# First-layer attention on one Trainium2 core: the four high and low products as 64-row pairs of heads, the folded causal mask, value products in twos

## The reference

```python
latent_kv = x @ w_kv_down                    # (4, 1024, 128)
kv = latent_kv @ w_kv_up                     # k and v, 16 heads of 64
q = (x @ w_q).reshape(Bx, Tx, 16, 64)
att = jnp.einsum('bqhd,bkhd->bhqk', q, k) * 64 ** -0.5
att = jnp.where(causal, att, -jnp.inf)
att = jax.nn.softmax(att, axis=-1)
y = jnp.einsum('bhqk,bkhd->bqhd', att, v)
return y.reshape(Bx, Tx, 1024) @ w_out
```

## Time and profile before

| | |
|---|---|
| median of 3 runs | 2570.04 us (2569.2 to 2572.35) |
| the profiled execution | 2569.28 us, its span 2567.5 us |
| PE busy in the span | 2312.1 us, 90% |
| DVE busy | 1850.8 us, 72% |
| ACT busy | 1497.5 us, 58% |
| granted TensorE clock, mean | 0.961 |

### The profile page before, as it was taken

The page is one execution under the profiler, slowest core; times in us unless marked ns, Lnnn a source line. Parts: engine busy times, 40 slices in busy tenths (PEclk is TensorE's granted clock), DMA queues, the critical chain, the costliest instruction groups (busy, mean ns, idle before and its releaser), DMA issues. The chain is left out here.

```text
span 2567.5 us, 46435 instructions
## 1 busy us (share of the span) xinstructions
PE 2312.1 (90%) x17339; PEld 1338.3 (52%) x17339; DVE 1850.8 (72%) x2346; ACT 1497.5 (58%) x2293; POOL 125.4 (5%) x256
## 2 busy tenths in 40 slices
PE   3799999999999999999999955859999999999998
PEld 2466666666565666666566632624444444444444
DVE  8677777777777777777777775067777777777781
ACT  3465666657575656666575731306666566566666
POOL 0100000000000000000000021000000000000000
PEclk8899999999999999999999977959999999999999
DMA  2000000000000000000000008033111110112000
GB/s 75 1 0 0 0 0 0 0 0 0 0 0 0 0 0 0 0 0 0 0 0 0 0 17 194 11 45 63 18 18 20 34 26 18 27 19 32 12 2 10
DMA packets 41099, 41.16 MB, mean 16 GB/s; under 512 B 21392, under 2 KB 33632, under 8 KB 40864
## 3 DMA queue, kind: packets, MB, share of 16 engines
q1 hardware_dynamic: 38904, 36.87, 7.2%
q10 hardware_dynamic: 1448, 1.61, 0.4%
q0 software_dynamic: 640, 1.15, 0.4%
HBM read 26.60 MB, written 11.63 MB: 15 GB/s over the span
## 5 line engine op out<-in xcount | busy, mean ns | idle before, releaser
L1462 DVE TENSOR_REDUCE nm_half<-slot 128x2 f32<-128x1024 f32 x512 | 605.2, 1223 | 188.4 <-PE slot L1311 146.2
L1444 ACT ACTIVATE pT<-slot 128x1024 f32<-128x1024 f32 x512 | 506.2, 1027 | 332.0 <-PE slot L1394 278.7
L573 ACT ACTIVATE probT<-slot 128x1024 f32<-128x1024 f32 x192 | 171.0, 890 | 326.9 <-PE slot L474 326.9
L474 PEld LDWEIGHTS slot<-ident,prob 128*128 128x128 f32 x2304 | 245.7, 141 | 198.6 <-issue 166.8
L610 DVE TENSOR_REDUCE negmax<-slot 128x1 f32<-128x896 f32 (+7 forms) x416 | 282.5, 708 | 76.4 <-PE slot L464 76.4
L474 PE MATMUL slot<-ident,prob 128*128 128x128 f32 x2304 | 328.0, 281 | 2.1
L486 PE MATMUL yspace<-probT,v_sb 128*64 128x512 f32 (+3 forms) x1536 | 318.3, 507 | 0.0
L1306 PE MATMUL slot<-ks,qs 48*128 48x512 f32 x1024 | 254.3, 495 | 53.6 <-DMA ks<-rows 29.1
L565 ACT ACTIVATE prob<-slot,negmax 128x896 f32<-128x896 f32 (+7 forms) x416 | 292.6, 720 | 9.6 <-DVE negmax L610 9.6
L1360 PE MATMUL yspace<-pT,v 128*32 128x512 f32 x2048 | 267.7, 604 | 1.7 <-ACT y_raw L1431 0.8
L459 PE MATMUL slot<-k_hi,q_st 128*128 128x512 f32 (+3 forms) x608 | 240.8, 396 | 26.4 <-ACT prob L565 11.4
(11 more groups left out here) (240 smaller groups left out, 3007.8 us busy)
## 6 DMA issues: line engine op xcount, KB each, us to landing
qs<-q_hi SPq DMA_DIRECT2D x64, 64.0 KB
qs<-q_lo SPq DMA_DIRECT2D x64, 64.0 KB
ks<-k_hi SPq DMA_DIRECT2D x60, 64.0 KB
ks<-k_lo SPq DMA_DIRECT2D x60, 64.0 KB
x_tok<-in_L_attn_x_dram SPq DMA_DIRECT2D x4, 512.0 KB, 7.4
q_hi<-qk_out SPq DMA_DIRECT2D x4, 512.0 KB, 3.2
q_lo<-qk_out SPq DMA_DIRECT2D x4, 512.0 KB, 4.1
k_hi<-qk_out SPq DMA_DIRECT2D x4, 512.0 KB, 4.2
```

The lines of the kernel that those rows point to most:

```text
L474: last = nc.tensor.transpose(ps[:, a * BANK + j * P:a * BANK + (j + 1) * P], prob[a][:, p_at(4 * c + j, kt)], ident[:, :])
L1444: nc.scalar.activation(pT[hp][m % PT_DEEP][:, :, :], slot[at["x", n] % RING][:, :].rearrange("p (j t) -> p j t", t=BANK), ACT.Exp)\
L1462: nc.vector.tensor_reduce(nm_half[:, h, :, p * TPB + i], slot[pos % RING][:, :].rearrange("p (a t) -> p a t", t=BANK), AX.X, ALU.max, nega ...
```

## The change

The high parts of both heads now stand side by side in one tensor, `q_hl[0]` (rows 0 to 63 head 0, rows 64 to 127 head 1), the low parts in `q_hl[1]`, and `k_hl` in the same way; nothing is doubled. A product of one head is over its own 64 rows, and the matmuls of the two heads are issued one after the other, on the two halves of the array's rows. Four passes (high and low of q with high and low of k) replace two of 128 rows. The mask is folded to 64 rows: `fold` picks and `causal` holds keys in two halves, so a tile's mask is two matmuls of 128 and 64 columns.

The tiles of i = 7 to 4 keep a space each but are computed in twos (both heads together, both spaces claimed first); for i = 3 to 0 both heads share one slot, head a in bank a, with one maximum (L615 of the new kernel) and two exponentials. `s_list` has 12 entries instead of 16; entries 3 and 7 are in `yspace`. LAG is 3, four buffers of `probT`, and products are issued in twos after items 3, 5, 7, 9 and 11 (`GROUP`); S_LEAD and S_PER are 2.

```diff
-                q_st = [sB(f"q_st{a}", [P, T], F32R) for a in range(2)]
-                k_hi2 = [sB(f"k_hi2{a}", [P, T], F32R) for a in range(2)]
-                k_lo2 = [sB(f"k_lo2{a}", [P, T], F32R) for a in range(2)]
+                q_hl = [sB(f"q_hl{r}", [P, T], F32R) for r in range(2)]
+                k_hl = [sB(f"k_hl{r}", [P, T], F32R) for r in range(2)]
...
-                NS = 2 * TPB
-                NS1 = NS // 2
+                s_list = [(i, a) for i in (7, 6, 5, 4) for a in range(2)] + [(i, None) for i in (3, 2, 1, 0)]
+                NS = len(s_list)
+                NS1 = TPB
...
-                LAG = 2
+                LAG = 3
+                GROUP = 2
...
-                S_LEAD, S_PER = 3, 5
+                S_LEAD, S_PER = 2, 2
...
-                Y_TILES = [0, 4, 8]
+                Y_TILES = [3, 7]
...
+                        def scores(n):
+
+                            i, a0 = s_list[n]
                             w = (i + 1) * P
+                            if n == 0:
+
+                                pe.wait_ge(hi_done, 2 * it + 2)
+                                freed(pe, it, TQ)
+                            if a0 is None:
+                                ps = score_claim(n)
+                                own_ps = [ps[:, a * BANK:a * BANK + w] for a in range(2)]
+                            else:
+                                own_ps = [score_claim(n + a)[:, 0:w] for a in range(2)]
+                            for k, (hq, hk) in enumerate(((0, 0), (1, 0), (0, 1), (1, 1))):
+                                if n == 0 and k == 2:
+
+                                    freed(pe, it, TK)
+                                for o in range(0, w, BANK):
+                                    m = min(BANK, w - o)
+                                    for a in range(2):
+                                        own = slice(a * HS, (a + 1) * HS)
+                                        last = nc.tensor.matmul(own_ps[a][:, o:o + m], q_hl[hq][own, i * P:(i + 1) * P], k_hl[hk][own, o:o + m],
+                                                                start=(k == 0), stop=(k == 3 and o + m < w))
+                                        if n == 0 and k == 0 and o == 0 and a == 0:
+
+                                            last.then_inc(proj_done, 1)
+                            for f in range(2):
+                                for a in range(2):
+                                    own = slice(a * HS, (a + 1) * HS)
+                                    last = nc.tensor.matmul(own_ps[a][:, i * P + f * HS:w], fold[own, f, :], causal[own, f, f * HS:P], start=False, stop=(f == 1))
+                                    if f == 1 and (a0 is not None or a == 1):
+                                        last.then_inc(score_space(n + a if a0 is not None else n)[1], 1)
+
+                        for n in range(0, NS1, 2):
                             scores(n)
...
-                            if m >= LAG:
-                                product(m - LAG)
-                        for m in range(NT - LAG, NT):
+                            if m >= LAG and m % GROUP == GROUP - 1:
+                                for k in range(GROUP):
+                                    product(m - LAG + k)
+                        for m in range(NT - LAG + GROUP - 1, NT):
                             product(m)
...
+                        for n, dst in ((TQ, q_hl), (TK, k_hl)):
+                            filled(act, it, n)
+                            nc.scalar.activation(dst[0][:, :], slot[n % RING][:, :], ACT.Copy).then_inc(hi_done, 1)
...
+                            for a, o in ([(a0, 0)] if a0 is not None else [(0, 0), (1, BANK)]):
+                                last = nc.scalar.activation(prob[a][:, p_at(i, 0, w)], ps[:, o:o + w], ACT.Exp, bias=negmax[:, i, a:a + 1],
+                                                            accum_out=sums[:, i, a:a + 1])
+                            last.then_inc(tile_free, 1)
...
+                        for k, (n, dst) in enumerate(((TQ, q_hl), (TK, k_hl))):
+                            dve.wait_ge(hi_done, 2 * it + k + 1)
+                            nc.vector.tensor_tensor(dst[1][:, :], slot[n % RING][:, :], dst[0][:, :].bitcast(F32), ALU.subtract).then_inc(free[n % RING], 1)
```

More of the change, by code:

```diff
@@ L73, in two_layers @@
             wdT = s0("wdT", [P, 3, C])
-            causal = s0("causal", [P, P], BF16)
+            fold = s0("fold", [P, 2, P], BF16)
+            causal = s0("causal", [P, 2, P], BF16)
             A = ExitStack()
@@ L95, in two_layers @@
                 pool_ready = sem("pool_ready")
+                fold_set = sem("fold_set")
                 ln_step = sem("ln_step")
@@ L302, in two_layers @@
                 assert TURNS == TILES and (TO + 1) % RING == 0
-                tiles_of = {1: [7, 6, 5, 4], 0: [3, 2, 1, 0]}
-                s_order = [(tiles_of[c][2 * k + r], a) for c in (1, 0) for k in range(2) for a in range(2) for r in range(2)]
                 H_OPS = 4 + FP4_OPS
@@ L438, in body, with score_claim @@
                         nc.tensor.matmul(ps[:, BANK:BANK + I], xq_s[:, :], wguT[:, I:2 * I], start=True, stop=True).then_inc(full[TGU % RING], 1)
[L440 to L447, removed]
+                        def score_claim(n):
                             ps, tile_full, tile_free = score_space(n)
@@ L454, in scores @@
                                 claim(at["s", n])
+                            return ps
+                        def scores(n):
+                            i, a0 = s_list[n]
                             w = (i + 1) * P
[L456 to L463, removed]
@@ L464, in scores @@
-                            nc.tensor.matmul(ps[:, i * P:w], identb[:, :], causal[:, :], start=False, stop=True).then_inc(tile_full, 1)
-                        for n in range(NS1):
+                            if n == 0:
[6 more added lines that the diff above has]
+                                own_ps = [score_claim(n + a)[:, 0:w] for a in range(2)]
@@ L588, in body @@
                     def body(b, g, it):
-                        own = lambda a: slice(a * HS, (a + 1) * HS)
-                        for a in range(2):
-                            dve.wait_ge(hi_done, 6 * it + a + 1)
-                            last = nc.vector.tensor_tensor(q_st[a][own(1 - a), :], slot[TQ % RING][own(a), :], q_st[a][own(a), :].bitcast(F32), ALU.subtract)
-                        last.then_inc(free[TQ % RING], 1)
-                        for a in range(2):
-                            dve.wait_ge(hi_done, 6 * it + 3 + 2 * a)
-                            last = nc.vector.tensor_tensor(k_lo2[a][own(a), :], slot[TK % RING][own(a), :], k_hi2[a][own(a), :].bitcast(F32), ALU.subtract)
-                            if a == 0:
-                                last.then_inc(lo_done, 1)
-                                dve.wait_ge(lo_done, it + 1)
-                            else:
-                                last.then_inc(free[TK % RING], 1)
-                                freed(dve, it, TK)
-                            nc.vector.tensor_copy(k_lo2[a][own(1 - a), :], k_lo2[a][own(a), :].bitcast(F32)).then_inc(qk_split, 1)
+                        for k, (n, dst) in enumerate(((TQ, q_hl), (TK, k_hl))):
+                            dve.wait_ge(hi_done, 2 * it + k + 1)
+                            nc.vector.tensor_tensor(dst[1][:, :], slot[n % RING][:, :], dst[0][:, :].bitcast(F32), ALU.subtract).then_inc(free[n % RING], 1)
@@ L613, in invert @@
+                            if a is None:
+                                nc.vector.tensor_reduce(negmax[:, i, :], ps[:, :].rearrange("p (a t) -> p a t", a=2)[:, :, 0:w], AX.X, ALU.max,
+                                                        negate=True).then_inc(neg_ready, 1)
+                            else:
+                                nc.vector.tensor_reduce(negmax[:, i, a:a + 1], ps[:, 0:w], AX.X, ALU.max, negate=True).then_inc(neg_ready, 1)
                         def invert():
```

35 lines of the change are left out of this document (16 added, 19 removed).

## The result

| | before | changed |
|---|---|---|
| median | 2569.94 us (20 runs, 2567.01 to 2573.34) | 2573.89 us (20 runs, 2570.68 to 2579.57) |
| ratio | 1 | 1.0017 (95% interval 1.001 to 1.0024) |
| span of the profiled execution | 2567.5 us | 2570.7 us |
| mean granted clock | 0.961 | 0.942 |

The account below looks back on a forecast made before the run. Each turn was taken as bound by the score loop, ACT tightest, up to t(1), then by PE. Terms -1.09 + 1.2 - 0.7 = -0.6 us a turn, 32 turns -19 us, gave 2550 us; range 2514 to 2590.

Parts of the forecast that it names:

- the likeliest case: Whole kernel: forecast of 2550 us, own range 2530 to 2564, clock staying at 1.00; chance 0.60.
- The rival's size: PE's idle 2 us before tile 4 halves the clock: up to 1.6 us a turn added, 2600 us; chance 0.07.
- the cancelling rival: Whole turn: handing over costs 1.8 us instead of 1.2, so gains and waits cancel, 2569 us; chance 0.12.
- Start of the scores: From Q to first scores: fewer copies and subtractions on ACT and DVE remove PE's two stops, -1.09 us a turn.
- Passes at nothing: Score matmuls: four 64-row pairs for both heads cost the same as two 128-row passes per head, 0 us.
- the rival feared: Narrow score passes: two successive weight loads set the pace, 0.216 us instead of 0.12, 2604 us; chance 0.09.
- The rival of exposed weight loads: Score passes: every weight load is exposed, 48 by 0.108 us, +4.6 us a turn, 2716 us; chance 0.02.
- Handing over in twos: Score stretch to t(1): paired tiles wait for two freed slots and ACT waits, +1.2 us a turn.
- Products in twos: After t(1): ten fewer transpose-product changes at 0.17 us, -1.7, against a 1.0 us wait; -0.7 us a turn.
- The wait at t(5): PE at transposes t(5) waits about 1.0 us for DVE's copy to free the slot of t(3).
- Sum: All terms of a turn together: -0.6 us, over 32 turns -19 us.
- PE's instructions: PE's instruction count in the whole kernel: rises by 74 x 32 to 19707.

Follow-up runs that it names:

- e2_twos: Kernel before with only the value products issued in twos (LAG 3, four buffers, GROUP 2), scores and mask as before; 2548.9 us.
- e1_fill: Changed kernel plus 18 throwaway bf16 matmuls of 128 columns on PE in the stop before tile 5's slot is free; 2537.5 us.
- e3_pairs: Changed kernel with the value products as in the kernel before (LAG 2, three buffers, no twos); 2575.49 us.
- e7_gap: Kernel before with one added wait: PE begins tile 4 only when exponential 2 has ended; 2629.62 us.
- e4_order: Changed kernel with the score tiles reordered so the third group needs one freed slot, and first transposes later; 2686.06 us.
- e5_split: Changed kernel with tiles 4 and 5 computed one head after the other, each when its own slot is free; 2540.86 us.
- e6_fill6: Changed kernel with 6 throwaway bf16 matmuls of 128 columns in PE's stop before tile 5's slot is free; 2540.05 us.

## Why the prediction was wrong

**The step that failed** is the choice of the likeliest case: the sum has the clock at nothing, and it measured 1.15 us a turn in 28 of 30 turns. The sum took every turn at the full 2.4 GHz ("Against it: the gap is shorter than the one shown to do it", chance 0.07). The stop came out at 1.94 us, as computed (about 2), and it was enough in 28 of 30 turns. The mistake was to hold a stop harmless because only one of 3.33 us was seen to do harm, with nothing between that and the stops of about 0.8 us; the rows bounded the matter on both sides and left this stop in the middle, which bears no chance of 0.07. The rival's size was a little too big: up to 1.6 us a turn, measured 1.15 (44.40 - 43.25). With this and the other terms 0.3 us a turn better than forecast, its 2600 us became 2574; that this is close to the cancelling rival's 2569 is chance, since its extra 0.6 us of handing over did not come.

**The other terms**, read from turns without a fall. ACT's first exponential, the first one of i = 5 and the first one of i = 3; then PE's first scores, third pair, t(1) and the next Q:

```profile
1383.39 1.11 ACT L578 ACTIVATE prob<-slot,negmax 128x1024 f32<-128x1024 f32 x1 [2.36 <-DVE negmax L618]
...
1388.64 0.91 ACT L578 ACTIVATE prob<-slot,negmax 128x768 f32<-128x768 f32 x1 [0.94 <-DVE negmax L618]
...
1392.29 0.69 ACT L578 ACTIVATE prob<-slot,negmax 128x512 f32<-128x512 f32 x1 [0.21 <-DVE negmax L615]
```

```profile
1379.89 2.11 PE L473 MATMUL slot<-k_hl,q_hl 64*128 64x512 f32 x16
...
1385.87 1.66 PE L473 MATMUL slot<-k_hl,q_hl 64*128 64x512 f32 x16 [1.94 <-ACT prob L578]
...
1395.83 2.88 PE L493 MATMUL slot<-ident,prob 128*128 128x128 f32 x24 [0.15 <-ACT probT L587]
...
1416.56 1.88 PE L427 MATMUL slot<-xnT,wq_s 128*128 x4
```

Windows over the first pairs of 512 and the last of 128 columns (us, busy PE, busy PEld, then the other engines as above):

```profile
846.70:848.61 1.91, 1.91 (x17) 1.62 (x17) 0.00 (x0) 1.11 (x2) 1.27 (x5) 1.00 0.00 0
862.86:863.37 0.51, 0.51 (x10) 0.51 (x10) 0.46 (x1) 0.51 (x1) 0.00 (x0) 1.00 0.00 0
```

- Start of the scores, forecast -1.09: from Q to the first score 7.74 us before, 6.59 after, -1.15. Right.
- Passes at nothing: right. Pairs over 64 rows run side by side: 8 pairs of 512 columns from 846.70 to 848.61, 0.24 each; 4 of 256 from 861.74 in 0.58; 4 of 128 from 862.86 in 0.51, 0.13 each with the entry. At 512 columns the loads lie under the matmuls. At 128 PEld is busy all the time, so there the loads may set the pace, but at 0.13 a pair and not at the 0.216 that the rival feared; the kernel before takes 0.28 for the two passes of one such tile (814.58 to 814.86), 0.56 for both heads, against 0.51 now. The rival of exposed weight loads is out. The rule of the Trainium skill, "TensorE: Matmul & The Clock Gate" (part on packing small matmuls), as the prediction applied it, is not borne out at 512 columns: two passes on the same rows, one after the other, show no load between them here.
- Handing over in twos, forecast +1.2: the scores to t(1) take 15.94 us (1395.83 - 1379.89) against 14.94, +1.00. ACT waits 0.94 us (forecast 1.0) and 0.21 (0.35). Right.
- Products in twos, forecast -0.7: from t(1) to the next Q 20.73 us (1416.56 - 1395.83) against 21.50, -0.77; alone, -0.67 (e2_twos). The wait at t(5) is 0.47 us in the changed kernel, 0.63 alone; forecast 1.0. The sum is right by two errors that cancel: with these waits taken out, ten changes fewer saved 1.24 us (0.77 + 0.47) or 1.30 (0.67 + 0.63), about 0.13 each, if nothing else changed there, and not 0.17.
- Sum, forecast -0.6: -0.92 at full clock (-1.15 + 1.00 - 0.77). With all turns at full clock the kernel takes 2537.5 us (e1_fill); the forecast of 2550 was right in direction for that kernel and short in size, by small errors of the same sign.
- PE's instructions: forecast 19707, measured 19387, 2048 more than before, or 64 a turn. I had counted 54 score matmuls a turn; with the tiles in `yspace` they are 64, and 128 after.

The balance of a turn: 44.17 - 0.92 + 1.15 = 44.40. Over the 30 turns after the first that adds up to 5.2 us; the first turn is 1.0 us longer, and the last turn's Q starts at 1460.97 us against 1454.91. The span is only 3.2 us longer. Most of the difference goes in front of the second attention, whose first matmul waits 23.22 us for the DMA of `ks` and not 29.12, and starts at 1689.82 us against 1689.13. That wait differs from run to run (23.2 to 29.7 us in the nine traces), and so blurs totals by some microseconds; the windows of a turn do not have it.

**Why one turn falls and the next does not.** The stops have the same length, yet the clock falls in 28 of 30 turns of 44.4 us, in 7 of 30 of about 44.05 (e3_pairs), in every second one in e7_gap, and always in e4_order. The end of the stop and the granted clock of the 1 us around the fall, early and late in the changed kernel:

```profile
230.95 2.17 PE L473 MATMUL slot<-k_hl,q_hl 64*128 64x512 f32 x16 [1.94 <-ACT prob L578]
...
1341.27 2.93 PE L473 MATMUL slot<-k_hl,q_hl 64*128 64x512 f32 x16 [1.94 <-ACT prob L578]
```

```profile
231.00:232.00 1.00, 1.00 (x10) 0.94 (x12) 0.57 (x1) 1.00 (x3) 0.00 (x0) 0.94 0.00 0
...
1341.00:1342.00 1.00, 0.73 (x4) 0.70 (x6) 0.88 (x1) 1.00 (x4) 0.00 (x0) 0.61 0.00 0
```

A mean of 0.94 puts the fall at 231.88 us, 0.93 after PE has resumed; 0.61 puts it at 1341.22, 0.05 before. In the 25 turns between, that distance shrinks steadily (0.43 at 852.67): the falls are 44.37 us apart, the turns 44.41. The turn after 1341.27 has no fall, and in the one behind it the fall is 0.84 us after the stop again; the same happened at 143.11 (0.03), 187.69 (none) and 230.95 (0.93). Across the turn without a fall the distance is 88.74 us, twice 44.37. So the falls keep a rhythm that is not the turn's, and the same stop brings one on or not according to where it lies in that rhythm. The other traces fit: in e3_pairs the seven falls lie between 0.06 us before and 0.20 after the end of the stop, in e7_gap from 1.16 after it (first) to 0.78 (last). The Trainium skill, "TensorE: Matmul & The Clock Gate", Part 1, says that the hardware's watch on activity is free-running; the trace of the changed kernel agrees, with 44.37 us against 44.41.

**What stays open.** How much idleness, and where, is enough for a fall, and why the half clock lasted 3.4 us in one case and 10.2 in another. No run was made that moves the stop alone and keeps the turn; e3_pairs changes the length of the turn and keeps the stop, but it also changes the order of the products. And the twos alone had one execution at a low mean clock (e2_twos).

## What to carry to other kernels

When a change makes PE hand over in larger pieces, write down PE's longest stop and its busy share around it, and treat a stop of 2 us as able to lower the clock, whatever the engines' balance says, and not only in the turn that you happen to read. In a trace, compare the granted clock turn by turn before looking for the loss elsewhere: two turns out of 30 without the fall priced it here to 0.1 us. The cure is cheap: a little work in the stop, thrown away (0.51 us of it sufficed, 2540 us) or real (e5_split, 2541 us), both 1.1 to 1.2% under the kernel before. e1_fill's 2537.5 us is no sign that more filling is better: its turns take the same 43.24 us as e6_fill6's, and 2.6 us of the difference is the wait for `ks` (24.81 us against 27.38).

## What the runs showed of the hardware that was not expected

- A stop of PE of 1.94 us, between stretches in which it is busy, was followed by about 3.4 us at half clock in 28 of 30 turns of the changed kernel and in 7 of 30 of e3_pairs. In the changed kernel these begin from 0.05 us before PE resumes to 0.93 us after, so mostly when it is working again (stop until 852.67, fall at about 853.1).
- The falls have a rhythm of their own: 44.37 us apart in a kernel whose turns take 44.41, until one turn is left out.
- After several short stops the clock halved 0.4 us into the next one, and stayed halved for 10.2 us a turn with PE busy for most of it (e4_order).
- Six bf16 matmuls of 128 columns, 0.51 us of work in the middle of the stop, keep 2.4 GHz in all turns (e6_fill6).
